# Window-attention feed-forward: GELU of a layer and sequence as one unit of three pieces, from three PSUM banks into three places

## The reference, cut to what matters

```python
def _layer(x, wqkv, qs, ksc, wo, lg, lb, w1, b1, w2, b2):
    ...
    x = x + o @ wo
    h = shift_token(x)
    mu = h.mean(-1, keepdims=True)
    var = h.var(-1, keepdims=True)
    h = (h - mu) / jnp.sqrt(var + 1e-05) * lg + lb
    h = h @ w1 + b1
    a, g = jnp.split(h, 2, axis=-1)
    h = a * jax.nn.gelu(g, approximate=False)
    x = x + h @ w2 + b2
    return x
for l in range(DEPTH):
    x = _layer(x, ...)
x = x + _L1_attn_ref(...) + _L1_ffn_ref(...)
```

## Time and profile before

| | us |
|---|---|
| median of 3 runs | 2607.62 (2605.55 to 2618.61) |
| the profiled execution, device time | 2598.73 |
| its span | 2597.4 |
| TensorE matmul busy | 1987.9 (77%) |
| VectorE (DVE) busy | 1942.8 (75%) |
| ScalarE (ACT) busy | 1920.3 (74%) |
| GpSimd (POOL) busy | 545.0 (21%) |
| ACT_TABLE_LOAD (L744), 199 of 1283 ns | 255.3 |

### The profile page before, as it was taken

The page is one execution under the profiler, slowest core; times in us unless marked ns, Lnnn a source line. Parts: engine busy times, 40 slices in busy tenths (PEclk is TensorE's granted clock), DMA queues, the critical chain, the costliest instruction groups (busy, mean ns, idle before and its releaser), DMA issues.

```text
span 2597.4 us, 32766 instructions
## 1 busy us (share of the span) xinstructions
PE 1987.9 (77%) x10866; PEld 1319.4 (51%) x10866; DVE 1942.8 (75%) x3005; ACT 1920.3 (74%) x2816; POOL 545.0 (21%) x206
## 2 busy tenths in 40 slices
PE   4776788876787887787777887788787877687666
PEld 2542466743454555454555555455454555455445
DVE  4889973479879875998788866899799956555644
ACT  3537677766798698886877778786878777788785
POOL 2512121121122121312212122312222022212210
PEclk9886899977879888897787978798788978787878
DMA  7722124422011001110111001110111000000000
GB/s 250 229 81 80 44 77 134 136 71 74 9 58 54 29 9 34 53 45 12 38 41 53 17 5 42 37 45 21 38 41 53 13 5 1 1 1 5 1 1 5
DMA packets 67528, 126.30 MB, mean 49 GB/s; under 512 B 8836, under 2 KB 40132, under 8 KB 67236
## 3 DMA queue, kind: packets, MB, share of 16 engines
q1 hardware_dynamic: 61808, 113.19, 13.5%
q0 software_dynamic: 2816, 7.21, 0.8%
q10 hardware_dynamic: 2740, 3.80, 0.4%
HBM read 111.33 MB, written 12.85 MB: 48 GB/s over the span
## 4 chain that ended last, share of the span: by engine, by line
PE 28%; DVE 28%; ACT 22%; issue 18%; DMA 2%; SPq 1%; DVEq 0%; ACTq 0%
DVE hB L1421 5%; PE ps L749 5%; ACT L744 4%; PE ps L928 4%; DVE hB L1415 3%; PE ps L970 3%; DVE n_c L1500 3%; DVE hB L1427 3%; ACT arena L1241 3%; PE ps L984 2%; ACT arena L1249 2%; ACT arena L1317 2%; PE ps L1054 2%; PE ps L1089 2%; PE ps L1029 2%
## 5 line engine op out<-in xcount | busy, mean ns | idle before, releaser
L1713 POOL TENSOR_TENSOR arena<-arena 128x2048 f32<-128x2048 f32 x64 | 304.4, 4756 | 1210.8 <-ACT arena L1243 1210.6
L749 PE MATMUL ps<-w_ident,arena 128*128 128x128 f32 x1647 | 302.8, 320 | 120.5 <-DVE arena L1564 21.6
L928 PE MATMUL ps<-hB,w_ident 128*128 128x512 f32 x512 | 316.3, 751 | 94.2 <-DVE hB L1427 93.2
L749 PEld LDWEIGHTS ps<-w_ident,arena 128*128 128x128 f32 x1647 | 230.0, 167 | 232.7 <-issue 155.4
L1421 DVE TENSOR_TENSOR_SCAN hB<-dA,hB 128x1024 f32<-128x1024 f32 x128 | 337.1, 2635 | 6.0 <-ACT dA L1205 5.2
L1717 POOL TENSOR_TENSOR arena<-arena,rb 128x1024 f32<-128x1024 f32 x64 | 154.9, 2420 | 559.0 <-DVE rb L1553 559.0
L744 ACT ACT_TABLE_LOAD x199 | 255.3, 1283 | 15.7 <-issue 12.1
L1205 ACT ACTIVATE dA<-dtv,w_A_log 128x510 f32<-128x510 f32 x256 | 169.4, 714 | 110.1 <-DVE hB L1421 108.5
L1029 PE MATMUL ps<-w_l_wqkv,arena 128*128 128x512 f32 x384 | 214.4, 675 | 21.0 <-ACT arena L1280 8.2
L1493 DVE TENSOR_SCALAR arena<-ps 128x512 f32<-128x512 f32 x256 | 163.8, 682 | 75.4 <-PE ps L970 73.6
L928 PEld LDWEIGHTS ps<-hB,w_ident 128*128 128x128 f32 x512 | 108.3, 232 | 209.4 <-issue 118.2
(11 more groups left out here) (198 smaller groups left out, 4288.0 us busy)
## 6 DMA issues: line engine op xcount, KB each, us to landing
BC<-bc_d SPq DMA_DIRECT2D x128, 512.0 KB
BC<-in_experts SPq DMA_DIRECT2D x31, 514.0 KB
arena<-in_experts SPq DMA_DIRECT2D x15, 514.0 KB
arena<-in_x SPq DMA_DIRECT2D x8, 256.0 KB, 5.4
xnT_d<-arena SPq DMA_DIRECT2D x8, 256.0 KB, 11.5
hB<-xnT_d SPq DMA_DIRECT2D x8, 256.0 KB
x<-in_x SPq DMA_DIRECT2D x8, 256.0 KB, 3.0
out<-go SPq DMA_DIRECT2D x8, 256.0 KB, 2.3
```

The costliest lines, as they stand in the source:

```text
L749: return t.transpose(out_, in_, ident[0:k, 0:k])
L928: e = t.matmul(lb(), ident, hB[k % 2][:, j], start=q == 0 and j == 0, stop=q == NQ - 1 and j == NG - 1)
L1713: g.tensor_tensor(la[m % 2], la[m % 2], cl, ALU.subtract).then_inc(g_sub, 1)
```

## The change

The unit `up` keeps only its TensorE stage. A new unit `gelu`, one for each layer and sequence, comes after all three `up` and makes the three GELU pieces one after another with a single `use(GELU)`, from the three banks into three places. Three new units `hid` do the VectorE multiplications, each freeing its `up` bank, and `down` comes after them. `up` 2 no longer comes after `up` 0, and the wait of ScalarE on the first multiplication ahead of the third piece is gone; `ga` has a third place, so `h2T` moves by one place in the arena. The list `LAYER` grows from 45 to 49 names.

```diff
-    "ln2": ..., "up": [("PE", 1.25), ("ACT", 0.38), ("DVE", 0.42)], "down": ...
+    "ln2": ..., "up": [("PE", 1.25)], "gelu": [("ACT", 1.15)],
+    "hid": [("DVE", 0.42)], "down": [("PE", 1.8), ("DVE", 0.4)],
...
-         ... "g_tan": "tan", "up": "gelu"}
+         ... "g_tan": "tan", "gelu": "gelu"}
...
-         "... oT0 oT1 wo ln ln2 lnT up0 up1 up2 down")
+         "... oT0 oT1 wo ln ln2 lnT up0 up1 up2 gelu hid0 hid1 hid2 down")
...
                     elif u == "up":
-                        x = [("lnT", n, b)] + [("up", n, b, k - 2) for z in range(1) if k == 2]
+                        x = [("lnT", n, b)]
+                    elif u == "gelu":
+                        x = [("up", n, b, z) for z in range(3)]
+                    elif u == "hid":
+                        x = [("gelu", n, b)]
                     elif u == "down":
-                        x = [("up", n, b, z) for z in range(3)]
+                        x = [("hid", n, b, z) for z in range(3)]
...
+    if u == "hid":
+        return (-1, ("up", n, b, k))
-    if u in BANKS and u != "ln":
+    if u in BANKS and u not in ("ln", "up"):
         return (-1, unit)
...
-            ga.append([qf[:, 4 * L:5 * L], qf[:, 5 * L:6 * L]])
-            h2T.append(qf[:, 6 * L:7 * L])
+            ga.append([qf[:, (4 + k) * L:(5 + k) * L] for k in range(3)])
+            h2T.append(qf[:, 7 * L:8 * L])
...
-                elif u == "up":
+                elif u == "gelu":
                     use(GELU)
-                    mm = HC[k]
-                    a.wait_ge(p_up[b], 3 * n + k + 1)
-                    if k == 2:
-                        a.wait_ge(v_hid[b], 3 * n + 1)
-                    a.activation(ga[b][k % 2][0:mm], lb()[0:mm, 0:L], ACT.Gelu, bias=f_b1[0:mm, l, 1, k:k + 1]).then_inc(a_ge[b], 1)
+                    for j, mm in enumerate(HC):
+                        a.wait_ge(p_up[b], 3 * n + j + 1)
+                        a.activation(ga[b][j][0:mm], bank(("up", n, b, j))[0:mm, 0:L], ACT.Gelu,
+                                     bias=f_b1[0:mm, l, 1, j:j + 1]).then_inc(a_ge[b], 1)
...
-                elif u == "up":
+                elif u == "hid":
                     mm = HC[k]
                     v.wait_ge(a_ge[b], 3 * n + k + 1)
-                    v.scalar_tensor_tensor(hid[b][0:mm, k], lb()[0:mm, L:2 * L], f_b1[0:mm, l, 0, k:k + 1], ga[b][k % 2][0:mm],
+                    v.scalar_tensor_tensor(hid[b][0:mm, k], bank(("up", n, b, k))[0:mm, L:2 * L], f_b1[0:mm, l, 0, k:k + 1], ga[b][k][0:mm],
                                            ALU.add, ALU.mult).then_inc(v_hid[b], 1)
```

More of the change, by code:

```diff
@@ L73 @@
     "oT": [("PE", 0.6), ("ACT", 0.5)], "wo": [("PE", 2.3), ("DVE", 0.4)], "ln": [("PE", 0.8), ("DVE", 0.8), ("ACT", 0.5)],
-    "ln2": [("DVE", 0.65)], "lnT": [("PE", 0.35), ("DVE", 0.45)], "up": [("PE", 1.25), ("ACT", 0.38), ("DVE", 0.42)], "down": [("PE", 1.8), ("DVE", 0.4)],
+    "ln2": [("DVE", 0.65)], "lnT": [("PE", 0.35), ("DVE", 0.45)], "up": [("PE", 1.25)], "gelu": [("ACT", 1.15)],
+    "hid": [("DVE", 0.42)], "down": [("PE", 1.8), ("DVE", 0.4)],
 }
@@ L79 @@
 NEEDS = {"e_ln": "ln", "e_route": "ln", "m_weights": "ln", "m_dt": "ln", "m_ex": "ln", "f_ln": "ln", "g_norm": "ln", "g_ln": "ln", "g_pow": "ln",
-         "norm": "ln", "score": "ln", "ln": "ln", "m_in": "silu", "g_tan": "tan", "up": "gelu"}
+         "norm": "ln", "score": "ln", "ln": "ln", "m_in": "silu", "g_tan": "tan", "gelu": "gelu"}
 SWITCH = 60.0
@@ L89 @@
 LAYER = ("shift qkv0 qkv1 qkv2 qkv3 qkv4 qkv5 norm qn0 heads0 qn1 heads1 score0 score1 pt0 pt1 pv0 pt2 pv1 pt3 pv2 on0 pv3 score2 score3 "
-         "pt4 pt5 pv4 pt6 pv5 on1 pt7 pv6 pv7 on2 oT0 oT1 wo ln ln2 lnT up0 up1 up2 down")
+         "pt4 pt5 pv4 pt6 pv5 on1 pt7 pv6 pv7 on2 oT0 oT1 wo ln ln2 lnT up0 up1 up2 gelu hid0 hid1 hid2 down")
 LAYER = [(x.rstrip("0123456789"), int(x[-1])) if x[-1].isdigit() and x != "ln2" else (x, 0) for x in LAYER.split()]
```

## The result

The changed kernel takes 2626.50 us, median of 5 runs (2625.57 to 2630.18), beside 2609.46 us (2605.55 to 2618.61) for the kernel before. The ratio is 1.0062, with a 95% interval of 1.0040 to 1.0085, about 16 us. (Ratios in this text are formed over all runs, so they differ a little from the quotient of the two medians.) Forecast was 2578. The profiled executions have spans of 2628.9 and 2597.4 us.

What follows compares the result with a forecast made beforehand. Three nearly equal engines handing work to each other bound the kernel, none alone. Only the loads counted, other terms zero: 2598.7 - 29 = 2569.7 us profiled, times 1.0034 = 2578 median; range for 8 in 10: 2540 to 2622.

Steps and rivals of the forecast that it cites:

- What bounds the kernel: Whole kernel: no engine is the limit; TensorE, VectorE and ScalarE, nearly equally busy, each stand about a quarter of the time.
- R1: Rival: loads gone, but the next engine replaces them on the chain; say 2602 us; chance 0.19, shared with another rival.
- Loads: ScalarE table loads around GELU: 49 go, 150 of 199 are left, 62.9 us less busy time at 1.283 us each.
- R4: Rival: each ScalarE switch also drains the pipe, doubling each load's price and the gain; about 2550 us; chance 0.02.
- How much of it is on the path: Share of the removed ScalarE loads that shortens the span: 29 us taken, between two weighings of 32.7 and 27.9.
- The chain: First weighing: 30 of 50 inner loads lie on the chain in order of time, 32.7 us, 52% of what is removed.
- the busy sum: Second weighing: span shrinks with the three engines' summed work, 62.9 / 5851 = 1.08%, 27.9 us.
- Latency of a feed-forward: First `up` to `down`: some 5 us go from each of 24 split feed-forwards; nothing counted beyond the loads.
- Banks: PSUM banks held by `up`: about equal in bank-time, peak one higher; zero in the sum.
- R3: Rival, slower: TensorE ahead of `score` lacks two adjacent banks while `up` holds three; 2633 us at 20 feed-forwards; chance 0.15.
- Due times and order: `LAYER` with 49 names makes first `up` due 8.6 us earlier and re-orders all five queues; zero, within 13 us either way.

Runs made afterwards that it cites:

- numbers 0, 1 and 2: Each kernel with due times moved at most 0.5 us by hash: before 1.0123, 1.0129, 1.0051; changed 1.0080, 1.0068, 1.0097 of the kernel before.
- the seven-bank runs: Planner given seven PSUM banks instead of eight: kernel before 1.0175, with hash number 0 1.0183; changed kernel 1.0380, with hash number 0 1.0401.
- before's variants: Kernel before with due times moved at most 0.5 us by hash numbers 144, 0, 1, 2: 1.0044, 1.0123, 1.0129, 1.0051, mean 1.0087.

## Why the prediction was wrong, step by step

**What bounds the kernel: right, and not taken seriously enough.** Three nearly equal engines hand work to each other, as the earlier trace rows say. One sentence beside it failed: "TensorE's busy time, the largest, doesn't change at all" (R1). The matmuls are the same, and they took 40.9 us longer. In such a kernel the order is worth as much as the work, and the forecast gave the order nothing.

**Loads: right.** 49 fewer were forecast and 51 are gone; ScalarE is busy for 1849 us and 1857 was forecast; L751 has 3% of the chain, as forecast. The switch costs its 1.283 us in busy time, and the 71 us that left ScalarE, 65.4 of them the loads, leave no room for the doubled price of R4.

**How much of it is on the path: too large.** The chain gave 0.52 and the busy sum 27.9 us; taken out alone the loads gave 18 us, 0.31 of their length. The chain names what was late at each point and not by how much it was later than the next, and the reduction for this in the sum, from 32.7 to 29, should have gone down to about 18 (11 to 26).

**Latency of a feed-forward: the step that failed in kind.** The forecast took the second load of the earlier trace rows away and left all else where it was, so `down` would come 5 to 8 us after the first `up`. In truth GELU now has one chance where it had three. Before, the first piece was offered as soon as the first `up` was done, and ScalarE switched when it next had nothing more urgent. Now the unit is offered once the third is done, and 13 of 32 then wait for over 10 us behind work on the Exp table, instead of 2. The mean to `down` went from 11.4 to 15.8 us. The delay is there in every order: with numbers 0, 1 and 2 the changed kernel has 7, 10 and 7 late ones and a mean of 14.0 to 14.8 us to `down`, and before has 3, 2 and 1 and 11.4 to 12.8. That the later offer is the reason is argued from the planner's rule; the delay itself is measured. What it costs in time isn't.

**Banks: wrong.** "In bank-time it is about equal" turned out as 527 and 1111 bank-us. It was reckoned for a GELU that comes at once. The earlier trace rows showed one that came after 23 us, and the prediction counted two of these as if their number would stay. R3 was right that the changed kernel needs its banks more: the seven-bank runs show it. Its path, stalls of TensorE ahead of `score`, isn't what happened with eight: that idle time fell from 39.9 to 27.6 us, and all of TensorE's by 9.4. That its 2633 lies near the measured 2626.5 is luck.

**Due times and order: the term of the sum that was mis-sized.** It was put at zero within 13 us "in either direction". With the work unchanged, due times alone cost 0.67%, and four re-orders by half a microsecond cost 0.4 to 1.3%, every one of them in the same direction. The bound was about half of what was seen, and centred on the wrong place: the order of before is better than its neighbours by 0.9% on the mean of four, so a change that makes the planner run again starts with some 23 us against it, unless its order is picked as well.

**The sum in hindsight.** The loads bring 18 us. The good order lost costs 23 (11 to 34 by single variants). That leaves 5 slower, and the measured 16 leave 11 for what the seven-bank runs and the bank count point to, the longer hold of three banks and the later `down`. The last item is a remainder, not a measurement, and the longer matmuls at a lower granted clock are a rival for it that no run rules out (12 us more than before's variants, on the mean); by the means of four (the change worth 3 us) it would be 15, and its error is as large as itself.

## What to carry to other kernels

Where a program orders the queues, a change of units, dependencies or due times is also a draw of a new order. Before the effect of the edit is read, run the kernel before with a few changes that mean nothing, to know how much the order alone is worth and whether the present one is a lucky one. Work gathered into one unit is offered once, when its last part is ready: count how long its buffers are held until then and behind what the one chance may queue, not only what the gathering saves.

## What the runs showed that I had not expected

- The same load of 1.283 us is worth 0.31 of itself taken out of one order and 1.33 of itself put into another (82 us for 61.6), there beside a granted clock of 0.805 for 0.819.
- The same 10866 matmuls took from 1987.9 us (mean granted clock 0.833) to 2062.8 us (0.810) in the twenty profiles, whose kernels differ in order, banks and table loads alone.
- Due times moved by at most 0.5 us, in a kernel of 2600 us, move the time by 0.4 to 1.3%, 11 to 34 us.
- One PSUM bank of eight is worth 16 to 46 us to the kernel before and 83 to 84 to the changed one.
